# Averages with exchanged operands and head sums in extra columns, value blocks in one zeroed bank

## The reference

```python
q, k, v = heads(x @ Wq), heads(x @ Wk), heads(x @ Wv)      # 16 heads of 8
scores = einsum('bhqd,bhkd->bhqk', q, k) * scale            # 32 queries, 32 keys
p = softmax(scores)            # L1Attn: softcap 50*tanh(s/50), then a causal mask
out = einsum('bhqk,bhkd->bqhd', p, v) @ Wo                  # L0Ffn: once for each of 4 experts
```

## Time and profile before

| what | value |
|---|---|
| median of three runs | 2164.21 us (2162.43 to 2166.15) |
| span of the profiled execution | 2160.1 us |
| PE busy over the span | 1764.0 us, 82% |
| DVE busy | 1435.0 us, 66% |
| ACT busy | 1016.2 us, 47% |
| POOL busy | 915.1 us, 42% |
| mean granted TensorE clock | 0.905 of full speed |

### The profile page before, as it was taken

One profiled execution on the slowest core, in us unless ns is written; L12 is line 12 of the kernel. 1 busy time (PEld: TensorE's weight loads), 2 busy tenths in 40 slices (PEclk: granted clock), 3 DMA queues, 4 the chain that ended last, 5 costly groups with the idle time before them and its releaser, 6 DMA issues.

```text
span 2160.1 us, 50856 instructions
## 1 busy us (share of the span) xinstructions
PE 1764.0 (82%) x20448; PEld 1176.2 (54%) x20448; DVE 1435.0 (66%) x3589; ACT 1016.2 (47%) x2574; POOL 915.1 (42%) x1083
## 2 busy tenths in 40 slices
PE   6678999899878789987578789998999896457496
PEld 4324557566544556643456656666676664135286
DVE  6799995688875665447970286565767666668622
ACT  5535764566644732242322365665666651124143
POOL 2243554455540514213522333137657567433433
PEclk9878999999999989999689999999999998757588
DMA  8000000100016100071033200100000000040187
GB/s 344 1 1 0 1 1 1 75 4 5 5 54 287 59 2 1 1 286 48 2 111 113 83 26 23 30 11 20 11 25 20 6 11 1 11 169 8 39 287 237
DMA packets 60427, 130.69 MB, mean 61 GB/s; under 512 B 16713, under 2 KB 38940, under 8 KB 54560
## 3 DMA queue, kind: packets, MB, share of 16 engines
q1 hardware_dynamic: 56896, 121.32, 15.7%
q0 software_dynamic: 3296, 6.12, 0.9%
HBM read 107.97 MB, written 20.12 MB: 59 GB/s over the span
## 4 chain that ended last, share of the span: by engine, by line
PE 48%; DVE 23%; issue 14%; ACT 7%; DMA 3%; SPq 2%; POOL 2%; POOLq 0%; DVEq 0%; ACTq 0%
PE PS L3230 4%; PE PS L2517 4%; PE PS L3277 3%; PE PS L424 3%; PE PS L3261 2%; PE PS L3219 2%; PE PS L3262 2%; DMA arena<-in_ctx 2%; PE PS L460 2%; DVE arena L1808 2%; PE PS L2317 2%; PE PS L4222 2%; PE PS L4231 1%; DVE arena L253 1%; PE PS L3269 1%
## 5 line engine op out<-in xcount | busy, mean ns | idle before, releaser
L321 POOL TENSOR_TENSOR arena<-arena 128x4 f32<-128x4 f32 (+3 forms) x109 | 118.7, 1090 | 396.5 <-DVE arena L264 260.0
L3345 ACT ACTIVATE arena<-PS,arena 128x289 f32<-128x289 f32 x256 | 128.0, 507 | 79.0 <-DVE arena L3459 78.1
L3230 PE MATMUL PS<-arena 128*128 128x289 f32 x512 | 153.4, 423 | 11.5 <-ACT arena L3345 7.5
L3459 DVE TENSOR_REDUCE arena<-PS 128x1 f32<-128x289 f32 x256 | 111.0, 453 | 75.2 <-PE PS L3230 70.0
L1872 POOL TENSOR_TENSOR arena<-arena 128x128 f32<-128x128 f32 x384 | 140.9, 405 | 43.1 <-PE PS L1735 18.9
L1258 POOL TENSOR_TENSOR arena<-arena 128x512 f32<-128x512 f32 x64 | 84.0, 1312 | 109.7 <-DVE arena L1403 109.7
L1808 DVE RECIPROCAL arena<-PS 128x128 f32<-128x128 f32 x96 | 91.6, 954 | 56.9 <-PE PS L1773 48.0
L1839 ACT COPY arena<-PS 32x128 f32<-32x128 f32 x384 | 99.7, 260 | 49.2 <-PE PS L1749 44.2
L3230 PEld LDWEIGHTS PS<-arena 128*128 128x128 f32 x512 | 87.9, 192 | 38.2 <-ACT arena L3345 19.6
L3188 POOL TENSOR_TENSOR arena<-arena 128x1024 f32<-128x1024 f32 x14 | 33.0, 2359 | 166.0 <-ACT arena L3336 166.0
L460 PE MATMUL PS<-arena 128*128 128x128 f32 (+4 forms) x576 | 84.9, 294 | 21.8 <-DVE arena L4338 7.8
(11 more groups left out here) (451 smaller groups left out, 4838.8 us busy)
## 6 DMA issues: line engine op xcount, KB each, us to landing
arena<-in_ctx SPq DMA_DIRECT2D x32, 1091.0 KB
arena<-in_f_w SPq DMA_DIRECT2D x39, 514.0 KB
arena<-in_ctx SPq DMA_DIRECT2D x16, 834.0 KB, 23.1
lists<-arena SPq DMA_DIRECT2D x8, 1040.0 KB, 10.6
arena<-in_f_w SPq DMA_DIRECT2D x32, 256.0 KB
arena<-in_ctx SPq DMA_DIRECT2D x16, 512.0 KB
arena<-in_mid SPq DMA_DIRECT2D x1, 3796.5 KB, 12.5
arena<-in_late SPq DMA_DIRECT2D x1, 3204.0 KB, 10.3
```

What stands on the lines that cost most here:

```text
L321: e.tensor_tensor(x, x, half.broadcast_to(list(x.shape)), ALU.pow).then_inc(*T.done("norm_root", tag))
L3230: e.matmul(PS[:, b, 0:UL], self.qt[i % 2][:, j, P * k:P * k + P], self.kt[i % 3][:, j, :], start=True, stop=True).then_inc(*T.done("k3_sco ...
L3345: e.activation(self.weights(n, k, 0, UL), PS[:, self.score_bank(n, k), 0:UL], ACT.Exp, bias=self.st[:, h, k:k + 1], accum_out=self.st[:, h ...
L3459: e.tensor_reduce(self.st[:, n % 2, k:k + 1], PS[:, self.score_bank(n, k), 0:UL], AXX, ALU.max, negate=True).then_inc(*T.done("k3_least", ...
```

## The change

`average` exchanges its operands: the turned weights (128x32) are stationary and the value block moves. The value block gets four more columns for each group and batch (36 in place of 32) that hold the constant `rowmask`, so the sum of each head comes out beside its average, and the matmuls with `headsum` go. The result now has queries on the partitions. DVE takes the reciprocal of 16 sums per partition, multiplies with the sum spread over 8 columns into a new tile `mean` (two buffers, signal `h_mean`); PE transposes it (`back`, between `scores(m)` and `values(m)`, for tile m-3, signal `h_back`), and ACT copies it from bank 7 into `OT` (`out`, at the head of its step, behind the tanh in L1Attn, signal `h_out`). Bank 4 is zeroed once ahead of the stream by four matmuls of a zero tile; values are written into all 512 columns of it, each head into its own columns, and ACT copies them with one instruction of 128x512 in place of four of 32x128. POOL writes the extra columns (three copies) and zeroes `mean[0]` in place of zeroing the three value blocks.

```diff
-    BANK = 5
+    BANK, WIDE = 5, S + HG
...
-        self.vB = [room.take(BT * D) for _ in range(3)]
+        self.vB = [room.take(BT * NG * self.WIDE) for _ in range(3)]
-        self.rest = [room.take(P) for _ in range(2)]
+        self.rest = [room.take(H) for _ in range(2)]
+        self.mean = [room.take(P) for _ in range(2)]
... (PE)
+            own = PS[:, 4, :].rearrange("p (j n h d) -> p j h n d", j=BT, n=NG, h=HG)
-                    k = e.matmul(PS[S * h:S * h + S, 4, S * j:S * j + S].rearrange("p (n d) -> p n d", n=NG),
+                    k = e.matmul(own[S * h:S * h + S, j, h],
                                  self.xT[:, P * i + S * j:P * i + S * j + S], wv[:, h], start=True, stop=True)
...
-            for j in range(BT):
-                for n in range(NG):
-                    r = slice(S * n, S * n + S)
-                    k = e.matmul(PS[r, 7, S * j:S * j + S], v[:, D * j + S * n:D * j + S * n + S],
-                                 p[:, P * n + S * j:P * n + S * j + S], start=True, stop=True)
             for n in range(NG):
-                k = e.matmul(PS[S * n:S * n + S, 7, P:2 * P], g.C["headsum"], p[:, P * n:P * n + P], start=True, stop=True)
+                for j in range(BT):
+                    a = NG * j + n
+                    k = e.matmul(PS[S * j:S * j + S, 7, w_ * n:w_ * n + w_], p[:, P * n + S * j:P * n + S * j + S],
+                                 v[:, w_ * a:w_ * a + w_], start=True, stop=True)
...
+        def back(m):
+            for w in T.due(("h_mean", (tag, m))):
+                e.wait_ge(*w)
+            e.transpose(PS[:, 7, 2 * P:3 * P], self.mean[m % 2], g.C["ident"]).then_inc(*T.done("h_back", (tag, m)))
+
+        for w in T.due(free[4], ("h_cleared", tag)):
+            e.wait_ge(*w)
+        for j in range(BT):
+            e.matmul(PS[:, 4, P * j:P * j + P], self.mean[0], g.C["ident"], start=True, stop=True)
 
         for m in range(self.N + 3):
             if m < self.N:
                 scores(m)
+            if 0 <= m - 3 < self.N:
+                back(m - 3)
+            if m < self.N:
                 values(m)
... (DVE)
-            e.reciprocal(rest, PS[:, 7, P:2 * P]).then_inc(*T.step())
-            for w in T.due(T.prev()):
-                e.wait_ge(*w)
-            e.tensor_tensor(self.OT[:, P * i:P * i + P], PS[:, 7, 0:P], rest, ALU.mult).then_inc(*T.done("h_out", (tag, m)))
+            e.reciprocal(rest.rearrange("p (n h) -> p n h", n=NG), both[:, :, S:]).then_inc(*T.step())
+            for w in T.due(T.prev(), ("h_back", (tag, m - 2))):
+                e.wait_ge(*w)
+            e.tensor_tensor(self.mean[m % 2].rearrange("p (n h d) -> p n h d", n=NG, h=HG),
+                            both[:, :, 0:S].rearrange("p n (h d) -> p n h d", h=HG),
+                            spread(rest.rearrange("p (n h) -> p n h", n=NG), [P, NG, HG, HD], 3),
+                            ALU.mult).then_inc(*T.done("h_mean", (tag, m)))
... (ACT)
-            for h in range(HG):
-                r = slice(S * h, S * h + S)
-                k = e.copy(v[r, :, h, :], PS[r, 4, 0:P].rearrange("p (a d) -> p a d", d=HD))
-            k.then_inc(*T.done("h_masked", (tag, m)))
+            e.copy(v, PS[:, 4, :].rearrange("p (a d) -> p a d", d=S)).then_inc(*T.done("h_masked", (tag, m)))
+
+        def out(m):
+            i = m % NT
+            for w in T.due(("h_back", (tag, m))):
+                e.wait_ge(*w)
+            e.copy(self.OT[:, P * i:P * i + P], PS[:, 7, 2 * P:3 * P]).then_inc(*T.done("h_out", (tag, m)))
... (POOL)
         for v in self.vB:
-            k = e.memset(v, 0.0)
-        k.then_inc(*T.done("h_cleared", tag))
+            v = v.rearrange("p (a w) -> p a w", w=self.WIDE)
+            e.tensor_copy(v[:, :, S:], spread(self.g.C["rowmask"], [P, BT * NG, HG], 1))
+        e.memset(self.mean[0], 0.0).then_inc(*T.done("h_cleared", tag))
```

More of the change, by code:

```diff
@@ L1833, in values @@
         def values(m):
-            v = self.vB[m % 3].rearrange("p (a h d) -> p a h d", h=HG, d=HD)
+            v = self.vB[m % 3].rearrange("p (a w) -> p a w", w=self.WIDE)[:, :, 0:S]
             for w in T.due(("h_values", (tag, m)), ("h_average", (tag, m - 3)), ("h_cleared", tag)):
                 e.wait_ge(*w)
-            for h in range(HG):
-                r = slice(S * h, S * h + S)
-                k = e.copy(v[r, :, h, :], PS[r, 4, 0:P].rearrange("p (a d) -> p a d", d=HD))
-            k.then_inc(*T.done("h_masked", (tag, m)))
+            e.copy(v, PS[:, 4, :].rearrange("p (a d) -> p a d", d=S)).then_inc(*T.done("h_masked", (tag, m)))
[4 more added lines that the diff above has]
+            e.copy(self.OT[:, P * i:P * i + P], PS[:, 7, 2 * P:3 * P]).then_inc(*T.done("h_out", (tag, m)))
         for m in range(self.N + 3):
+            if m >= 3 and self.softcap is None:
+                out(m - 3)
             if m < self.N:
@@ L1850, in act @@
                     scale, before = self.softcap, "h_tanh"
+                    if m >= 3:
+                        out(m - 3)
                 values(m)
@@ L1854, in act @@
                 e.activation(p, p, ACT.Exp, scale=scale).then_inc(*T.done("h_exp", (tag, m)))
+            elif self.softcap is not None:
+                out(m - 3)
             if 0 <= m - 1 < self.N and self.softcap is None:
```

4 lines of the change are left out of this document (2 added, 2 removed).

## The result

The kernel before takes 2163.32 us (median of 4 runs, 2160.76 to 2166.15), the changed one 2140.06 (4 runs, 2135.56 to 2145.08). The ratio is 0.9904, with a 95% interval of 0.988 to 0.9929: the medians lie 23 us apart and the ratio stands for 21 (15 to 26), where 39 were forecast. The profiled execution has a span of 2139.2 us against 2160.1.

What follows compares the result with a forecast made beforehand. PE and DVE, both near 90% of a four-tile L0Ffn group, were taken to pace tiles by handing over. L0Ffn with the start -27, L1Attn -4.5, L3Ffn -7.5 made -39 us: 2125 us, range 2108 to 2150.

Steps and rivals of the forecast that it cites:

- The transpose back: PE, each tile: one transpose more takes 0.10 us, from four that take 0.42.
- The wait that is added: PE waits in `back` for `h_mean`: 0.69 us, just covered in L0Ffn by 0.77; some 0.26 open in L1Attn and L3Ffn.
- one of the prediction's own signs of being wrong: PE at `back`: the forecast is wrong if PE idles there by half a microsecond.
- the period of L0Ffn: Four tiles fall from 13.83 to 12.2 us, set by PE and the subtraction-to-scores loop; 19 us for 12 groups.
- The last expert: End of L0Ffn, without projections: DVE sets the pace, each of 16 tiles gives 0.55 us, 9 us in all.
- L1Attn: This stream gains 4.5 us, bounds 0 and 9: 0.70 saved in 8 tiles, 0.26 lost in 4.
- L3Ffn: This stream gains 7.5 us, bounds 2 and 11: DVE sets the pace in some 11 of 16 tiles, 0.70 each.
- A: Rival: the division isn't covered by the scores, `back` costs PE 0.45 us a tile; gain 15 us, 2149; chance 0.17.
- B: Rival: shape changes stall PE at each `back` in the short streams, 32 x 0.20 = 6.4 us lost; 2132; chance 0.10.
- C: Rival: reciprocal (25 us) and head sums (12.7) leave the chain whole, other parts at upper bounds; -56 us, 2108; chance 0.08.
- D: Rival: `back` is not covered at all and drains on both sides, 0.99 us a tile; 37 us slower, 2201; chance 0.05.
- E: Rival: reciprocal keeps most of its 0.95 us or bank 5 gives the gain back; within 4 us of 2164; chance 0.04.

Runs made afterwards that it cites:

- the two halves: Kernel before with only the value blocks changed: 2165.81 us, ratio 1.0018; changed kernel with the value blocks made as before: 2138.59 us, ratio 0.9898.
- the other execution: The changed kernel, not altered, run a second time on the chip: 2139.64 us, ratio 0.9899 to the kernel before.
- e12_values_halved: Changed kernel with a tile's value blocks made by 8 matmuls of 64 columns in place of 16 of 32: ratio 0.9866, first 48 L0Ffn tiles 155.34 us.

## Why the prediction was right or wrong

*The reciprocal* was right: 0.26 us against 0.25 taken, and 88 elements take 0.71, by the same fixed part and slope. The strided PSUM source shows no price (256 ns against 254 from SBUF). *The multiplication* is 0.29, as taken. *The copies on ACT* are right (0.586 and 0.268), and that they lie beside other work is shown by the two halves.

*The averages*: the 36 columns cost nothing to speak of (201 ns a matmul, 199 before), and from the average to the next scores it is 0.40 us, 0.04 under what I took.

*The transpose back* was mis-sized. I priced it at 0.10, a quarter of four in a row; alone, between the mask and the values, it holds PE for 0.26 (457.93 to 458.26 is mask, 458.26 to 458.52 the transpose). The second one in the kernel with two costs just the 0.10. So PE's tile is 2.41 and not 2.28. But this is not where the time went: without the transpose the kernel gains 4 us.

*The wait that is added* is where the prediction had it. In L0Ffn it is covered: PE waits at `back` three times in 64 tiles, 2.1 us in all. In L1Attn it is open in 15 of 16 tiles, and with 0.55 us on the mean it is twice the 0.26 that I took (8.2 us in all, the longest 1.5, where the sum has 4 x 0.26 = 1.0). That is half a microsecond, one of the prediction's own signs of being wrong. PE's waits in L1Attn:

```profile
PE PS L1780 <- DVE arena L1824: 8.2, 15, 1.5
```

*The start*: the zeroing takes 1.06 us ahead of L0Ffn, as forecast. The 2.8 us of the profile are not its price: the other execution has the same zeroing and stands at -0.1.

*The time as a whole* came within the range, 2140 in 2108 to 2150, 15 us above the likeliest value. *The step that failed* is the period of L0Ffn: "the last 1.3 us is one waiting for the other", and that four tiles would fall to PE's own work and a loop of 12.2. I had counted durations on both engines, and nothing that limits how fast PE gets its instructions. The group of 13.83 us that I took was a short one; the twelve have a mean of 14.01. That was close to the floor by supply already (65.9 instructions a us, floor 13.6), so taking 0.70 us a tile off DVE alone brings only 5 us of 168 (the reciprocal cut). The rest of what the change got in L0Ffn, 8.9 of 14.1 us when it comes second, goes with what I held to be small: 7 matmuls a tile fewer on PE (8 of the head sums away, one transpose added), 14 instructions, 14 x 14.8 ns = 0.2 us, 0.8 for four tiles, 13.6 to 12.8. Neither part has the gain by itself: with the long reciprocal put back the same saving of instructions brings nothing, since PE then waits at `back`. My number for four tiles was 12.2, the measured 12.83; the kernel that has 32 instructions less and the same work reaches 12.35. I hold this for the gap over the first 48 tiles; of the changed kernel's 5.4 us of idle PE there, 3.3 are stops without a releaser and 1.7 are waits for DVE.

*The last expert* gave 5.6 and 4.2 us where I took 9. No experiment was cut for it. In most of them it moves with the instruction count (51.1 before, 50.1 to 50.4 with the reciprocal cut, 45.5 to 46.9 changed, 42.2 with the values left out). PE's stops without a releaser there are 3.2 us before, 8.6 with the reciprocal cut, 2.7 in the changed kernel and none with the values left out. Against it: the rate there is only 59 to 64 instructions a us, and the kernels without `back` (47.6) and with it in pairs (48.1) are slower than the changed one with no more instructions. So the supply may have a part in it; the cause stays open.

*L1Attn* came out, -3.8 for -4.5, but in part by luck, since the wait in it was mis-sized eightfold. The wait costs little beyond what else PE would wait for: in the kernel without `back` PE stops there for 7.6 us without a releaser, and the stretch takes 46.96 us for 46.51.

*L3Ffn* gave half of the forecast. Two things are seen there. The first is its end, whose 8.8 us marked "remote" the prediction left as they are. From the first to the fourteenth reciprocal the changed kernel gained 4.6 us, and 5.1 in the other execution; in the last two intervals it lost 1.3 in both (17.6 us for 16.3). Before, the 8.8 us stood ahead of the last reciprocal. Now 6.8 us of the kind stand ahead of the last but one (the row at 1994.71), and the last comes another 6.0 behind it, after 5.3 of waiting for PE. What holds DVE there no run isolates. The second is the clock. Its granted clock was 0.71 from 1941 to 2021 us before and 0.63 from 1923 to 2001 after:

```profile
1923.00:2001.00 78.00, 57.52 (x1483) 42.13 (x1479) 49.75 (x169) 30.11 (x65) 34.07 (x59) 0.63 0.05 17
```

PE is busy for 57.5 us there with 1483 matmuls, where 1560 had taken 54.0: fewer matmuls, and each longer. In the other execution the clock was 0.66 and the stretch 76.5. So part of what DVE gave may have gone into a slower PE; how much, stays open, since no run held the clock of this stretch fixed.

*L1Cross* and the stretch ahead of L0Ffn: the profile showed 4.0 and 2.8 us of loss in code that isn't changed. The second execution has 1.5 and none, with a granted clock of 0.96 for 0.89 in L1Cross. I had left this variation out of the sum.

*The rivals.* A (PE waits half a microsecond at `back`) names a time near the result, but not by its mechanism: there is no such wait in L0Ffn, only in L1Attn, which kept its gain. Its 0.45 a tile was not derived from any row. B's shape changes show in no idle time of PE at the transpose beside its wait. C and E did not come; C's parts as named add up to 57 us and not 56. D did not come either, but the margin that kept it away is small, as the long reciprocal shows.

## What to carry to other kernels

Where a stage consists of many short matmuls, count PE's instructions (each f32 matmul is two matmuls and two weight loads here, a transpose one of each) and divide by the time: at 67 to 68 a us the engine waited for its program here, its busy share looked full, and work taken off PE or DVE hardly came back as time unless instructions went with it. Look for idle times without a releaser in the middle of a group, and count the instructions between them. And a wait that fits under other work should be given with its margin: here the margin was some 0.1 us, and 0.75 us more on the far side turned a gain of 1% into a loss of 1.8%.

## What the runs showed of the hardware that I had not expected

- PE's instructions come as packets of 16 KB for 256 of them, one every 3.8 us on the mean where PE takes them fastest (68 recorded instructions a us over 48 tiles), and PE stops there for 0.2 to 1.4 us in the middle of a group, at multiples of 127 matmuls with their loads. Fewer moving columns don't help: 448 fewer per tile, 162.9 and 163.7 us for 48 tiles. At 57 instructions a us (`e12_values_halved`) there is no such stop.
- Half of the sixteen 128x32 value matmuls, with the other two of four column groups empty, take 0.37 us against 0.39 for all; the columns of all sixteen in half as many matmuls of 64 take 0.57.
- Four f32 matmuls with 2 moving columns hold PE for 0.34 us between two 128x128 groups.
- A 128x128 f32 transpose holds PE for 0.26 us alone behind the mask matmuls and for 0.10 more as the second of two.
- With the transpose left out PE fell to half clock around 435 and 575 us, where the changed kernel stayed at 1.00 in the profile of the result (0.96 over the last expert in its other execution). Ahead of the first it had stopped for 1.1 us with nothing to wait for; in 570 to 575 us it was busy for 63%. With the sums cut it fell to half clock around 561 us, behind a stop of 1.0 us.
